# A value product in three rounded products, one period later, and two products of a recurrence moved to GpSimd

## The reference

```python
a  = LN(x)                                   # the residual is taken from here
xk, xv, xr = (shift(y) * (1 - m) + y * m for m in mixes)      # y = LN(a)
k, v, r = xk @ w_key, xv @ w_value, sigmoid(xr @ w_recept)
# recurrence over the 512 tokens, for each of 256 channels:
out_t   = (alpha_{t-1} + e^{..} v_t) / (beta_{t-1} + e^{..})
alpha_t = e^{..} alpha_{t-1} + e^{..} v_t ;  beta_t = e^{..} beta_{t-1} + e^{..}
x  = a + (r * out) @ w_output
z  = LN(x)
h  = relu(mix(z) @ f_w_key) ** 2             # 1024 hidden channels
x  = x + sigmoid(mix(z) @ f_w_recept) * (h @ f_w_value)      # the value product
```

## Time and profile before

| | |
|---|---|
| time, 3 runs | median 1428.28 us (1426.02 to 1428.88) |
| span of the profiled execution | 1423.3 us, 28011 instructions |
| TensorE busy | 1341.5 us (94%) |
| VectorE / ScalarE / GpSimd busy | 905.0 / 683.0 / 629.5 us |
| granted TensorE clock, mean | 0.968 |

### The profile page before, as it was taken

How to read it: one execution, slowest core, us unless ns; L and a number is a source line. 1 busy time by engine, 2 the same in 40 slices (tenths; PEclk the granted TensorE clock), 3 DMA queues, 4 the chain that set the end, 5 groups by cost and what they waited for, 6 DMA issues and landing times. The chain is left out here.

```text
span 1423.3 us, 28011 instructions
## 1 busy us (share of the span) xinstructions
PE 1341.5 (94%) x7638; PEld 1132.6 (80%) x7639; DVE 905.0 (64%) x2171; ACT 683.0 (48%) x1541; POOL 629.5 (44%) x583
## 2 busy tenths in 40 slices
PE   6999997799999999966899999998979999999997
PEld 4999986688888888834777777777868888888886
DVE  5877888454444444457888898887864454444443
ACT  4576765233333333354687669766643333333332
POOL 4768663355555555424132222222213555555553
PEclk9999997999999999998999999999989999999999
DMA  8575853566665333370000000000326766633333
GB/s 274 209 266 196 296 206 134 167 161 163 167 158 116 52 54 58 45 225 0 1 16 31 0 30 30 30 0 31 120 89 176 169 158 161 167 71 58 54 52 42
DMA packets 100874, 157.86 MB, mean 111 GB/s; under 512 B 10256, under 2 KB 60688, under 8 KB 100816
## 3 DMA queue, kind: packets, MB, share of 16 engines
q1 hardware_dynamic: 73120, 118.67, 24.5%
q0 software_dynamic: 27264, 37.82, 16.6%
q10 hardware_dynamic: 432, 0.66, 0.1%
HBM read 95.89 MB, written 61.21 MB: 110 GB/s over the span
## 5 line engine op out<-in xcount | busy, mean ns | idle before, releaser
L1367 POOL DMA_INDIRECT out_x<-second_y,second_add_token x71 | 112.7, 1587 | 154.0 <-DMA out_x<-second_y,second_add_token 71.4
L1367 POOL DMA_INDIRECT x_rows<-first_y,first_add_token x70 | 111.3, 1590 | 150.4 <-ACT first_y L1405 88.8
L1358 POOL DMA_INDIRECT xs<-normed_rows,gather_token x140 | 140.5, 1004 | 45.9 <-issue 41.5
L1475 DVE TENSOR_TENSOR first_hT_lo<-bank,first_hT_hi 128x512 fp32r<-128x512 f32 x71 | 49.1, 692 | 159.9 <-ACT first_hT_hi L1395 159.9
L1475 DVE TENSOR_TENSOR second_hT_lo<-bank,second_hT_hi 128x512 fp32r<-128x512 f32 x71 | 49.1, 692 | 158.1 <-ACT second_hT_hi L1395 155.8
L166 PE MATMUL bank<-ring,first_xT_hi 128*128 x284 | 118.9, 418 | 3.4 <-DVE first_xT_lo L1463 3.4
L166 PE MATMUL bank<-ring,second_xT_hi 128*128 x284 | 118.9, 419 | 2.2 <-DVE second_xT_lo L1463 2.2
L168 PE MATMUL bank<-ring,first_xT_lo 128*128 x284 | 112.9, 398 | 0.0
L168 PE MATMUL bank<-ring,second_xT_lo 128*128 x284 | 112.8, 397 | 0.0
L167 PE MATMUL bank<-ring,first_xT_hi 128*128 x284 | 112.6, 397 | 0.0
L167 PE MATMUL bank<-ring,second_xT_hi 128*128 x284 | 112.4, 396 | 0.0
(11 more groups left out here) (455 smaller groups left out, 3909.0 us busy)
## 6 DMA issues: line engine op xcount, KB each, us to landing
ring<-split_weights SPq DMA_DIRECT2D x192, 256.0 KB, 3.1
a_wraw<-in_L_ffn_w SPq DMA_DIRECT2D x21, 512.0 KB, 6.3
split_weights<-a_whi SPq DMA_DIRECT2D x21, 512.0 KB, 2.6
split_weights<-a_wlo SPq DMA_DIRECT2D x21, 512.0 KB, 3.5
normed_rows<-xg SPq DMA_DIRECT2D x16, 528.0 KB, 3.1
...
```

Source lines behind the costliest of these rows:

```text
L1358: nc.gpsimd.indirect_dma_start(xs[q][:], None, normed_dram[:], bass.IndirectOffsetOnAxis(ap=gather_token[q][:], axis=0)).then_inc(loaded[q ...
L1367: nc.gpsimd.indirect_dma_start(x_dram[:], bass.IndirectOffsetOnAxis(ap=add_token[q][:], axis=0), y[q], None, compute_op=ALU.add).then_inc( ...
L1475: nc.vector.tensor_tensor(hT_lo[par][:].rearrange("p k t -> p (k t)"), th_bank[par][:], hT_hi[par][:].rearrange("p k t -> p (k t)").bitcas ...
```

## The change

1. **Value product.** The weights are halved as before and then split into `fv_hi` (fp32r, ScalarE) and `fv_lo` (fp32r, GpSimd). `hidden` writes Relu and Square to `hT_raw` and gets a third pass for each tile, a Copy that rounds to `hT_hi`. GpSimd's `low_hidden` makes `hT_lo`, two tiles at a time. TensorE multiplies hi by hi and hi by lo (`value_hi`, 32 products for a half), then lo by hi (`value_lo`, 16).
2. **Place.** Both halves of the value product of b-1 now stand in period b, between the projections of b+1 and the key products of b. Nothing of it is left behind the receptance product, except in period 7. The second tile of the r projection moves behind the transposes of the second norm. `finish(b-1, 0)` moves from the end of VectorE's period to the place of `finish(b-1, 1)`.
3. **Recurrence.** `dv` and the first `num` product go from VectorE to GpSimd (`decayed_value`, `first_value`); `add_mixed` moves forward on GpSimd and both `add_channel(b-1, .)` stand behind them.
4. **Buffers.** `dv`, `num`, `gT` and `den` take the places of k, v, v and rho, `al` that of eps; in the routing 4 buffers for rows stand where 6 were, and 4 for sent blocks.
5. ScalarE takes `row_exp` later, and the transposed second norm ahead of the gaps.

```diff
@@ -1817,9 +1823,11 @@
                 wait_count(act, vk_done, 2 * b)
                 for m in range(FCH):
                     act.wait_ge(fk_done, FCH * b + m + 1)
-                    nc.scalar.activation(hT[:, m, :], xb_[m % 4][:], ACT.Relu).then_inc(h_relu, 1)
+                    nc.scalar.activation(hT_raw[:, m, :], xb_[m % 4][:], ACT.Relu).then_inc(h_relu, 1)
                     act.wait_ge(h_relu, FCH * b + m + 1)
-                    nc.scalar.activation(hT[:, m, :], hT[:, m, :], ACT.Square).then_inc(h_ready, 1)
+                    nc.scalar.activation(hT_raw[:, m, :], hT_raw[:, m, :], ACT.Square).then_inc(squared, 1)
+                    act.wait_ge(squared, FCH * b + m + 1)
+                    nc.scalar.activation(hT_hi[:, m, :], hT_raw[:, m, :], ACT.Copy).then_inc(h_ready, 1)
 
             def receptance(b):
 
...
             nc.scalar.activation(wo_s[:], wo_s[:], ACT.Copy, scale=0.5).then_inc(halved, 1)
-            nc.scalar.activation(fv_s[:], fv_s[:], ACT.Copy, scale=0.5).then_inc(halved, 1)
+            nc.scalar.activation(fv_raw[:], fv_raw[:], ACT.Copy, scale=0.5).then_inc(halved, 1)
+            act.wait_ge(halved, 2)
+            nc.scalar.activation(fv_hi[:], fv_raw[:], ACT.Copy).then_inc(fv_hi_ready, 1)
 
             def period(b):
                 if has_before(b, 2):
...
@@ -1874,16 +1884,13 @@
                 if has_next(b, 1):
                     evacuate_k(b + 1)
                 norm2(b)
+                if has_next(b, 1):
+                    evacuate_v(b + 1)
+                evacuate_xn2(b)
+                if has_next(b, 1):
+                    gaps_of_step(b + 1)
                 if has_before(b, 2):
                     row_exp(b - 2)
-                if has_next(b, 1):
-                    evacuate_v(b + 1)
-                if static(b, 0):
-                    evacuate_xn2(b)
-                if has_next(b, 1):
-                    gaps_of_step(b + 1)
-                if not static(b, 0):
-                    evacuate_xn2(b)
                 if has_next(b, 1):
                     weights_of_step(b + 1)
                     evacuate_r(b + 1)
...
 
+            def low_hidden(b, m):
+
+
+                wait_apart(pool, h_ready, FCH * b + m + 2, passed["pool"])
+                raw = hT_raw[:, m:m + 2, :]
+                nc.gpsimd.tensor_tensor(hT_lo[:, m:m + 2, :], raw, hT_hi[:, m:m + 2, :].bitcast(F32), ALU.subtract).then_inc(h_lo_ready, 1)
+
+            def decayed_value(b):
+
+
+                wait_apart(pool, kvr_evac, 6 * b + 4, passed["pool"])
+                wait_apart(pool, expd, 6 * b + 3, passed["pool"])
+                wait_apart(pool, rho_ready, b + 1, passed["pool"])
+                nc.gpsimd.tensor_tensor(dv[:], d2[:], v[:], ALU.mult).then_inc(dv_ready, 1)
+
+            def first_value(b):
+
+                wait_apart(pool, expd, 6 * b + 6, passed["pool"])
+                wait_apart(pool, dv_ready, b + 1, passed["pool"])
+                nc.gpsimd.tensor_tensor(num[:], rho[:], v[:], ALU.mult).then_inc(first_ready, 1)
+
+            pool.wait_ge(fv_hi_ready, 1)
+            nc.gpsimd.tensor_tensor(fv_lo[:], fv_raw[:], fv_hi[:].bitcast(F32), ALU.subtract).then_inc(fv_lo_ready, 1)
+
             def period(b):
                 rstd(mv2, shift2, own_2, var2_ready, rstd2_ready, b)
+                if has_before(b, 1):
+                    low_hidden(b - 1, FCH - 2)
+                add_mixed(b)
                 if has_next(b, 2):
                     rstd_in(b + 2)
+                if has_next(b, 1):
+                    decayed_value(b + 1)
+                    first_value(b + 1)
                 if has_before(b, 1):
+                    add_channel(b - 1, 0)
                     add_channel(b - 1, 1)
+                low_hidden(b, 0)
+                if has_before(b, 1):
                     rstd(mvg, shiftg, own_c, varg_ready, rstdg_ready, b - 1)
-                if has_next(b, 1):
-                    wait_apart(pool, num_ready, b + 2, passed["pool"])
-                add_mixed(b)
-                add_channel(b, 0)
+                for m in range(2, FCH - 2, 2):
+                    low_hidden(b, m)
 
             over_periods(pool, period)
+            low_hidden(B - 1, FCH - 2)
+            add_channel(B - 1, 0)
             rstd(mvg, shiftg, own_c, varg_ready, rstdg_ready, B - 1)
             first_gather(nc, pool, gathered, normed_dram, stored)
 
         @block.vector
         def _(dve):
...
-                dve.wait_ge(kvr_evac, 6 * b + 4)
-                dve.wait_ge(expd, 6 * b + 3)
-                r_.link(nc.vector.tensor_tensor(dv[:], d2[:], v[:], ALU.mult))
                 dve.wait_ge(expd, 6 * b + 4)
-
-            def denominator(b):
-
                 for i in range(KC):
-                    last = nc.vector.tensor_tensor_scan(be[:, i, 1:N + 1], d1[:, i, :], d2[:, i, :], 0.0, ALU.mult, ALU.add)
-                dve.wait_ge(expd, 6 * b + 6)
-                nc.vector.tensor_tensor(num[:], rho[:], v[:], ALU.mult)
+                    last = nc.vector.tensor_tensor_scan(be[:, i, :], d1[:, i, :], d2[:, i, :], 0.0, ALU.mult, ALU.add)
                 r_.link(last)
-                nc.vector.tensor_tensor(den[:], rho[:], be[:, :, 0:N], ALU.add)
 
             def numerator(b):
 
+                dve.wait_ge(dv_ready, b + 1)
                 for i in range(KC):
-                    last = nc.vector.tensor_tensor_scan(al[:, i, 1:N + 1], d1[:, i, :], dv[:, i, :], 0.0, ALU.mult, ALU.add)
+                    last = nc.vector.tensor_tensor_scan(al[:, i, :], d1[:, i, :], dv[:, i, :], 0.0, ALU.mult, ALU.add)
+                dve.wait_ge(first_ready, b + 1)
+                nc.vector.tensor_tensor(den[:, :, 1:N], rho[:, :, 1:N], be[:, :, 0:N - 1], ALU.add)
                 r_.link(last)
-                r_.link(nc.vector.tensor_tensor(num[:], num[:], al[:, :, 0:N], ALU.add))
...
                     begin(b + 2)
+                mix_channel(b)
+                low_key(b)
                 if has_before(b, 2):
                     softmax_end(b - 2)
                 if static(b, B - 1):
                     dve.wait_ge(top_taken, B - 2)
                     early_choices(nc, placing, route, idx, const)
-                mix_channel(b)
-                low_key(b)
                 if has_before(b, 1):
+                    finish(b - 1, 0)
                     finish(b - 1, 1)
-                if has_next(b, 1):
-                    decayed_value(b + 1)
                 if has_next(b, 1):
                     denominator(b + 1)
                     numerator(b + 1)
@@ -2209,9 +2247,9 @@
                     for n in range(4):
                         hot_blocks(nc, dve, route, const.lane, n)
                         hot_rows(nc, dve, route, const.lane, n)
-                finish(b, 0)
 
             over_periods(dve, period)
+            finish(B - 1, 0)
             for n in range(4, EARLY):
...
@@ -2315,26 +2353,28 @@
                 pe.wait_ge(xg_ready, b + 1)
                 transposes(xg, round_gate(b))
 
-            def value_tile(out, src, j):
+            def value_hi(b, h):
+
+
+                if has_next(b, 2):
+                    pe.wait_ge(kvr_evac, 6 * b + 15 + h)
+                pe.wait_ge(h_relu, FCH * b + FCH)
+                pe.wait_ge(h_ready, FCH * b + FCH)
+                for j in range(2):
+                    for i in range(FCH):
+                        out, part = xb_[2 + h][:, j * C:(j + 1) * C], hT_hi[:, i, (2 * h + j) * P:(2 * h + j + 1) * P]
+                        nc.tensor.matmul(out, part, fv_hi[:, i, :], start=(i == j == 0), stop=False, skip_group_check=True)
+                        nc.tensor.matmul(out, part, fv_lo[:, i, :], start=False, stop=False, skip_group_check=True)
+
+            def value_lo(b, h):
+
                 for i in range(FCH):
-                    last = nc.tensor.matmul(out[:, j * C:(j + 1) * C], src(i, j), fv_s[:, i, :], start=(i == 0), stop=(i == FCH - 1))
-                return last
-
-            def value_product(b, h):
-
-
-                if h == 1:
-                    if has_next(b, 2):
-                        pe.wait_ge(kvr_evac, 6 * b + 16)
-                    pe.wait_ge(h_relu, FCH * b + FCH)
-                pe.wait_ge(h_ready, FCH * b + FCH)
-                if static(b, B - 1) and h == 0:
-                    value_tile(xb_[2], cut(hT, 0), 0)
-                    gate_transposes(b - 1)
-                    value_tile(xb_[2], cut(hT, 0), 1).then_inc(vk_done, 1)
-                    gate_products(b - 1)
-                else:
-                    token_product(xb_[2 + h], cut(hT, h), fv_s, FCH).then_inc(vk_done, 1)
+                    if i % 2 == 0:
+                        pe.wait_ge(h_lo_ready, FCH // 2 * b + i // 2 + 1)
+                    for j in range(2):
+                        last = nc.tensor.matmul(xb_[2 + h][:, j * C:(j + 1) * C], hT_lo[:, i, (2 * h + j) * P:(2 * h + j + 1) * P],
```

(23 more changed lines are left out.)

74 lines of the change are left out of this document (43 added, 31 removed).

## The result

The changed kernel takes 1491.44 us (median of 4 runs, 1490.85 to 1493.04), the one before 1428.58 (4 runs): 1.0447 times as long, 95% interval [1.0432, 1.0461], +62.9 us. That is within the predicted range, 9 us above the forecast. The profiled execution of the changed kernel has a span of 1491.3 and a time of 1493.04, 1.75 us apart. If the same 1.75 us held before (its record has no time for that execution), the other 3.3 of the 5.0 us that the prediction put between median and span were a profiled execution faster than the median.

A forecast was written before the change was run, and what follows sets the result against it. TensorE bounded the kernel; now ScalarE's tail would hold it: 6 x (53.9 - 46.9) = +42, period 0 zero, end +12, so 1423.3 + 54 = 1477.3 span, plus 5.0 to the median: 1482 us, range 1460 to 1498.

The forecast's parts named there:

- ScalarE's tail exposed: Steady periods: TensorE idles 7.8 us each ahead of the transposes of xg, waiting for ScalarE; chance 0.67.
- Arithmetic of the value product: TensorE's value product: 96 fp32r products take 11.2 us against 13.88, 2.7 us less in a period.
- The copy: ScalarE's hidden: a tile goes from 1.15 to 1.81 us, hidden from 9.2 to 14.5.
- The place of the value product: Ahead of xg's transposes: TensorE has 11.3 us of work, ScalarE 19.1, so 7.8 idle; period 52.0 us.
- The clock: TensorE behind each idle stretch: 1.2 GHz costs 1.9 us, making the period 53.9; bounds nothing to 1.9.
- The recurrence's products and GpSimd: Loop from gT to gT through the value product: 46.3 to 53.6 us, just under ScalarE's loop, adding nothing.
- The small parts: fv_hi and fv_lo, row_exp, split r projection, buffers: each at most 1.5 us without cover, taken as zero.
- Period 0: First period, TensorE waiting for gT instead: between 4 us less and 2 more, taken as zero.
- Period 7 and behind it: End of the phase: finish(7, 0) 44.7 us behind TensorE's start instead of 32.9; +12 us (10 to 13).
- Rival B: GpSimd and VectorE exclude each other throughout and their sum bounds: 58.4 us a period, 1509 us; chance 0.12.
- Rival A: TensorE stays the bound in steady periods: period 44.2 us, 19 us faster, 1409 us; chance 0.06.

The follow-up runs named there:

- experiment 4: Changed kernel with the whole value product in float32 in its new place, no Copy and no low parts, recurrence products still on GpSimd: 1470.21 us, ratio 1.0301.
- experiment 1: Changed kernel without the Copy, Square writing its rounded result straight into hT_hi: 1480.02 us, ratio 1.0376.
- the filled kernels: Changed kernel, with the Copy and without it, TensorE's idle stretches filled with matmuls without use: 1481.76 us with the Copy, 1471.69 without.
- Experiment 7: Changed kernel with GpSimd's low part of the value weights delayed until VectorE has made the mixes of sequence 1: 1487.65 us, ratio 1.0426.
- experiment 8: Against the changed kernel: only the second value half in fp32r, first half float32 in its old place, recurrence products on VectorE: 1442.90 us; with further edits 1434.94, then 1423.11.
- experiment 2: Changed kernel with dv and the first num product back on VectorE: 1493.84 us with the Copy, 1488.26 without it.
- the last kernel: Final kernel of experiment 8: second value half alone in fp32r, high key part ahead of step weights, earlier row buffers and end: 1423.11 us, ratio 0.9966.

## Why the prediction was right

The time was in the range and the main step, ScalarE's tail exposed, was seen as forecast. But part of the nearness is luck. The sum for the span was 1477.3, and the span came out at 1491.3, 14 us more; the 5.0 us added to get from span to time were 3.3 more than this kernel's 1.75 and brought the forecast nearer. Against the sum, the start of the phase had 6.1 us more, periods 1 to 6 had 5.0 more (47.1 for 42), the end 4.6 more (16.6 for 12), and period 0 had 2.8 less.

- *Arithmetic of the value product*: right at 0.117 us a product. The whole took 11.65 instead of 11.2, as its first product stands 0.52 us ahead of the second: 2.2 us saved, not 2.7.
- *The copy*: 1.81 us a tile, as worked out.
- *The place of the value product*: right. 6.90 us idle for 7.8. ScalarE's tail took 18.9 for 19.1; TensorE had 0.9 more work, as its last key tiles step at ScalarE's pace. The side remark that even a free copy leaves 2.5 us came out at 2.72 (experiment 4, in float32). So the loss was forecast by the right wait, but that wait was not the only one that would have held: with it shortened by 5.3 us the period kept 53.8 of 54.4 us (experiment 1).
- *The clock*: right in kind, 2.5 us for 1.9 by the rows, since b_wo now stands in the stretch at 1.2 GHz; filling it gave back 2.1 in the mean, because the second chain then holds.
- *The recurrence's products and GpSimd*: its loop was put between 46.3 and 53.6 and "just under the other one". gT ended 1.6 us ahead of b_wo (923.68, 925.31) in 54.5, so 52.9, and the remark that it would keep the loss if the copy were cheaper is what experiment 1 shows. But the path was drawn too simply: within 0.7 us of the value product, ScalarE's high key part is late as well, and in the filled kernels it is the one that holds. The Trainium skill (SBUF — State Buffer, section "SBUF: two separate sides") says that a VectorE instruction with two SBUF inputs and a GpSimd instruction that reads SBUF exclude each other for whole instructions. The trace agrees: 3.42 us for 1.22 beside a GpSimd row of 2.94, and 6.55 unchanged for the reciprocal, which has one input.
- *The small parts*, taken at zero, is the step that failed. It took fv_lo to lie where "TensorE waits for the recurrence of sequence 0", and forgot that the exclusion it had just used makes that very recurrence late. The two products took 4.3 us longer (6.62 for 2.31), and b_wo of sequence 0 started 6.1 us later, 1.5 of it because the phase itself began later. Experiment 7 gives back the 4.3 in the rows. That "the split r projection costs nothing" failed in period 1 (below); and the four row buffers of the routing do not stand in the sum at all, while experiments 4 and 8 show a wait of 5.68 us for one of them.
- *Period 0* within its bounds (-2.8). Period 1 was taken as steady (+7) and is +11.0: TensorE waits 2.18 us for the second norm there. With the r projection split it asks for that norm 1.7 us earlier; and what GpSimd makes for the norm is ready 8.8 us behind the start of the period, against 7.0 before.
- *Period 7 and behind it*: +14.4 and +2.1 for +12. The sum up to finish(7, 0) left out the clock behind the wait for the last rounded tile: TensorE stops 3.53 us there, and the 32 high products of the first half take 5.4 us instead of 3.7, at a mean granted clock of 0.69. The low parts are done at 1081.5, 8 us before TensorE asks for them, so GpSimd doesn't hold here. Further on VectorE waits 0.85 us for a row buffer and TensorE 6.6 for ScalarE's blocks; experiment 8 prices buffers and end together at 11.8 us for another kernel.
- *Rival B* (1509) holds in a weaker form than it was put: VectorE's busy time rose by 8.8 us over the 39.3 that it had left, and with the clock restored VectorE was busy 49.1 of 52.5 us. But its own sum, 58.4 us a period, was not reached, and two GpSimd rows less changed nothing (experiment 2). *Rival A* is excluded by every kernel here with the whole product in fp32r.

Not settled: how the 43 us of experiment 4 divide between place, shared buffers, ScalarE's order and GpSimd's products; and whether the gain of the last kernel needs fp32r at all.
